# First pair's copy by DMA ahead of the norm, scaled in place; Fourier steps between the chunks of conv1

## The reference

```python
for j in range(4):
    z = conv3x3(x, Kj); z = batchnorm(z, gamma[j], beta[j]); z = relu(z)
    z = conv3x3T(z, Kj)
    x = batchnorm(x + 0.1 * z, gamma[j], beta[j])
    x = diag_imp_conv_fft(x, Lj, 0.1)      # fft2, times a real table per channel, ifft2
```

## Time and profile before

| what | value |
| --- | --- |
| median of 3 runs | 698.69 us (698.69 to 700.88) |
| the profiled execution | 700.2 us, span 698.4 us |
| TensorE (PE) busy | 619.7 us, 89% |
| VectorE (DVE) busy | 493.7 us, 71% |
| ScalarE (ACT) busy | 343.7 us, 49% |
| GpSimd (POOL) busy | 233.3 us, 33% |

### The profile page before, as it was taken

One profiled execution on the slowest core, in us unless ns is written; L12 is line 12 of the kernel. 1 busy time (PEld: TensorE's weight loads), 2 busy tenths in 40 slices (PEclk: granted clock), 3 DMA queues, 4 the chain that ended last, 5 costly groups with the idle time before them and its releaser, 6 DMA issues.

```text
span 698.4 us, 14578 instructions
## 1 busy us (share of the span) xinstructions
PE 619.7 (89%) x5840; PEld 200.9 (29%) x5840; DVE 493.7 (71%) x875; ACT 343.7 (49%) x640; POOL 233.3 (33%) x180
## 2 busy tenths in 40 slices
PE   6498999999999979999898899998978989989783
PEld 4122333222332223233232222332222223323221
DVE  2679888865786785738868767486778554867674
ACT  1466666652894322419932314299223233982232
POOL 0367666771142432202225222022252220222200
PEclk9699999999999999999999999999999999999988
DMA  9995111117600022294000224930004159000044
GB/s 187 182 168 97 32 32 33 31 31 161 157 1 1 1 63 62 70 224 116 1 2 1 70 55 107 224 79 1 2 1 109 30 133 218 3 2 1 1 123 120
DMA packets 44786, 51.21 MB, mean 73 GB/s; under 512 B 36528, under 2 KB 36656, under 8 KB 42672
## 3 DMA queue, kind: packets, MB, share of 16 engines
q1 hardware_dynamic: 40240, 48.99, 32.8%
q10 hardware_dynamic: 4480, 1.30, 1.2%
HBM read 11.99 MB, written 4.19 MB: 23 GB/s over the span
## 4 chain that ended last, share of the span: by engine, by line
PE 54%; ACT 20%; DVE 14%; issue 6%; DMA 3%; SPq 1%; POOL 0%; DVEq 0%; ACTq 0%; POOLq 0%
PE psum L1025 29%; ACT Z L613 10%; PE psum L1097 6%; ACT work L635 6%; PE psum L1164 3%; PE psum L1048 3%; DVE Z L950 2%; DMA X<-X 2%; PE psum L1221 2%; PE psum L1193 2%; PE psum L1236 2%; DVE work L923 2%; PE psum L1085 2%; DVE work L968 2%; DVE work L933 1%
## 5 line engine op out<-in xcount | busy, mean ns | idle before, releaser
L1025 PE MATMUL psum<-X,wts 128*32 128x512 f32 x1536 | 171.3, 594 | 9.1 <-DMA X<-X 5.0
L1025 PE MATMUL psum<-Z,wts 128*32 128x512 f32 x1536 | 172.3, 594 | 4.3 <-DVE Z L890 4.3
L474 POOL TENSOR_TENSOR Z<-X 128x512 f32<-128x512 f32 x64 | 80.8, 1286 | 251.2 <-DVE X L908 251.2
L635 ACT ACTIVATE work<-X,small 128x512 bf16<-128x512 f32 x128 | 90.7, 710 | 87.7 <-DVE X L908 87.7
L550 ACT ACTIVATE Z<-psum 128x512 f32<-128x512 f32 x64 | 38.2, 596 | 140.4 <-PE psum L1025 129.3
L484 POOL TENSOR_TENSOR X<-Z 128x1024 f32<-128x1024 f32 x24 | 56.9, 2394 | 113.0 <-DVE Z L950 113.0
L810 DVE BATCH_NORM_STATS2 stats<-Z 128x6 f32<-128x512 f32 x60 | 41.0, 691 | 69.7 <-ACT Z L550 69.6
L1025 PEld LDWEIGHTS psum<-Z,wts 128*32 128x32 f32 x1536 | 50.1, 109 | 115.5 <-issue 106.9
L613 ACT ACTIVATE Z<-Z,small 128x512 f32<-128x512 f32 (+4 forms) x92 | 80.3, 922 | 5.2 <-DVE small L880 4.7
L1025 PEld LDWEIGHTS psum<-X,wts 128*32 128x32 f32 x1536 | 47.8, 109 | 121.4 <-issue 109.8
L908 DVE SCALAR_TENSOR_TENSOR X<-psum,X 128x512 f32<-128x512 f32 x64 | 44.2, 690 | 36.2 <-PE psum L1025 36.0
(11 more groups left out here) (127 smaller groups left out, 819.5 us busy)
## 6 DMA issues: line engine op xcount, KB each, us to landing
X<-X SPq DMA_DIRECT2D x64, 260.0 KB, 3.9
Z<-Z SPq DMA_DIRECT2D x32, 520.0 KB, 9.2
Z<-x SPq DMA_DIRECT2D x36, 128.0 KB, 4.1
out<-Z SPq DMA_DIRECT2D x24, 128.0 KB, 2.4
parS<-par SPq DMA_DIRECT2D x4, 673.0 KB, 11.8
Z<-x SPq DMA_DIRECT2D x12, 120.0 KB, 5.1
Z<-x ACTq DMA_DIRECT2D x14, 64.0 KB, 4.3
Z<-x SPq DMA_DIRECT2D x14, 64.0 KB, 4.7
```

Of the source, the lines that this page charges most:

```text
L474: nc.gpsimd.tensor_tensor(rows(Z0, REG, bp, CH * (2 * half + i), CH), low, high, op=op)\
L635: nc.scalar.activation(by_row(rest[:, o:o + N // 2].bitcast(bf16)), xc, what, bias=small[:, 26:27], accum_out=sums[:, NCH * i + c:NCH * i ...
L1025: last = nc.tensor.matmul(out_b[C * r:C * r + C, :], weights[:, o:o + C], rows(src, reg, bp, g, CH, dj - 1), start=(dj == 0), stop=(dj == ...
```

## The change

- SP copies pair 0 to X2 (layers 1 to 3) as soon as GpSimd has unmixed it, before the second norm is known, so the copy is unscaled.
- ScalarE then scales X0 of pair 0 in three parts, and with the first and the last the one edge row group of X2 that holds half of the partitions (`scale_first`). VectorE scales the other rows of X2 in three parts (`scale_copy`, steps `copied`). Chunks 0 to 2 of conv1 wait for one part of each.
- conv1 follows the norm and the last two quarters of forward H of pair 2. Inverse W of pair 1 lies ahead of the moments; the return of slot 0 and inverse H of pair 2, and all of pair 3, move between the chunks of conv1.
- In conv2 the return of slot 0 goes behind the following chunk, inverse H of pair 1 and forward W of pair 2 change places, VectorE's scaling becomes a step of its own (`scaled`), and ScalarE's sums of chunks are put off by a table (`SUMS`).
- The weights of conv1 (`prepare((0,))`) are made behind chunk 13 of conv2, those of conv2 in the step `weights`.
- GpSimd's last mixing of a layer waits until the second norm is known.
- The last layer keeps the order behind conv2 (`last_steps`), with the changes in conv2.

```diff
@@ def fourier
     if what == "fwdH":
-        steps = [("slot0", j, bp)] + steps + [("slot0c", j, bp)]
+        steps = [("slot0", j, bp)] + steps + [("scaled", j, bp)]
@@ def layer_steps
-        9: fourier(j, 1, "fwdW"),
+        9: [("slot0c", j, 0)] + fourier(j, 1, "fwdW"),
         10: fourier(j, 0, "invH"),
         11: fourier(j, 1, "fwdH"),
-        12: fourier(j, 0, "invW") + [("back", j, 0)],
-        13: fourier(j, 2, "fwdW"),
-        14: fourier(j, 1, "invH"),
-        15: fourier(j, 2, "fwdH"),
+        12: [("slot0c", j, 1)] + fourier(j, 0, "invW") + [("back", j, 0, 0), ("back", j, 0, 1)],
+        13: fourier(j, 1, "invH"),
+        14: fourier(j, 2, "fwdW"),
...
-    steps += [("moments", j), ("norm", j, 2), ("affine", j, 0), ("turn", j, BP - 1), ("weights", j)]
-    steps += fourier(j, 1, "invW") + [("back", j, 1)] + fourier(j, 3, "fwdW") + fourier(j, 2, "invH")
+    if j + 1 == DEPTH:
+        return steps + last_steps(j)
+    steps += quarters("fwdH", j, 2, (0, 1)) + [("slot0", j, 2), ("scaled", j, 2, 0)] + fourier(j, 1, "invW")
+    steps += [("moments", j), ("norm", j, 2)] + quarters("fwdH", j, 2, (2, 3))
+    steps += [("affine", j, 0), ("copied", j, 0), ("back", j, 1, 0), ("copied", j, 1), ("back", j, 1, 1), ("copied", j, 2)]
+    steps += [("scaled", j, 2, 1), ("turn", j, BP - 1), ("weights", j)]
     rest = {
-        0: [("affine", j, 1)],
-        1: fourier(j, 3, "fwdH"),
-        2: fourier(j, 2, "invW") + [("back", j, 2)],
-        3: fourier(j, 3, "invH"),
-        5: fourier(j, 3, "invW") + [("back", j, 3), ("affine", j, 2)],
+        0: [("slot0c", j, 2)],
+        2: fourier(j, 2, "invH") + [("affine", j, 1)],
+        3: fourier(j, 3, "fwdW"),
+        4: fourier(j, 2, "invW") + [("back", j, 2, 0), ("back", j, 2, 1)],
+        5: fourier(j, 3, "fwdH") + [("affine", j, 2)],
+        6: [("slot0c", j, 3)] + fourier(j, 3, "invH"),
+        7: fourier(j, 3, "invW") + [("back", j, 3, 0), ("back", j, 3, 1)],
         9: [("affine", j, 3)],
     }
+SUMS = {c: (c,) for c in range(5)} | {6: (5,), 8: (6,), 9: (7,), 10: (8,), 11: (9, 10), 12: (11,), 13: (12, 13), 14: (14,), 15: (15,)}
@@ SP
+                        elif bp == 0:
+                            sp.wait_ge(parts_added, 2 * BP * (j - 1) + h + 1)
@@ GpSimd, mix_halves
+                if bp == BP - 1 and i == 1 and j + 1 < DEPTH:
+                    pool.wait_ge(bn_ready, 2 * j + 2)
@@ ScalarE
+            def scale_first(j):
+                for h in range(2):
+                    act.wait_ge(x2_in[0][h], 32 * (j + 2))
+                for g, n in ((0, CH), (CH, CH), (2 * CH, 2 * CH)):
+                    parts = [(X0, REG, g, n, 0, 128)]
+                    if g == 0:
+                        parts.append((X2, REG2, 0, 1, 2 * C, 128))
+                    if g + n == G:
+                        parts.append((X2, REG2, G, 1, 0, 2 * C))
+                    for t, reg, first, many, p0, p1 in parts:
+                        z = rows(t, reg, 0, first, many, 0, p0, p1)
+                        last = nc.scalar.activation(z, z, ACT.Identity, bias=small[p0:p1, 13:14], scale=small[p0:p1, 12:13])
+                    last.then_inc(x_back, n // CH)
@@ VectorE
+            def scale_copy(j, i):
+                dve.wait_ge(bn_ready, 2 * j + 2)
+                for h in range(2):
+                    dve.wait_ge(x2_in[0][h], 32 * (j + 2))
+                g, n = ((1, CH), (1 + CH, CH), (1 + 2 * CH, G - 1 - 2 * CH))[i]
+                z = rows(X2, REG2, 0, g, n)
+                nc.vector.tensor_scalar(z, z, S(12), S(13), ALU.mult, ALU.add).then_inc(copy_scaled, 1)
...
                         dve.wait_ge(bn_ready, 2 * j + 2)
-                        prepare()
+                        prepare((1,))
...
                         elif at[1] == 13 and j + 1 < DEPTH:
                             sum_kernels(j + 1)
+                            prepare((0,))
@@ TensorE
-                    pe.wait_ge(weights_ready, j + 1)
+                    pe.wait_ge(weights_ready, 2 * j if j else 1)
-                if c % Q < 2:
+                if j and c < 3:
+                    pe.wait_ge(x_back, NCH * (j - 1) + (1, 2, 4)[c])
+                    pe.wait_ge(copy_scaled, 3 * (j - 1) + c + 1)
+                elif c % Q < 2:
```

More of the change, by code:

```diff
@@ L156, in layer_steps, with last_steps @@
     for c in range(NCH):
-        if j + 1 < DEPTH:
-            steps.append(("conv1", j + 1, c))
-        steps += rest.get(c, [])
-    return steps
+        steps += [("conv1", j + 1, c)] + rest.get(c, [])
+    return steps
+def last_steps(j):
+    steps = fourier(j, 2, "fwdH") + [("slot0c", j, 2), ("moments", j), ("norm", j, 2), ("affine", j, 0), ("turn", j, BP - 1)]
+    steps += fourier(j, 1, "invW") + [("back", j, 1, 0), ("back", j, 1, 1)] + fourier(j, 3, "fwdW") + fourier(j, 2, "invH")
+    steps += [("affine", j, 1)] + fourier(j, 3, "fwdH") + [("slot0c", j, 3)] + fourier(j, 2, "invW")
+    steps += [("back", j, 2, 0), ("back", j, 2, 1)] + fourier(j, 3, "invH") + fourier(j, 3, "invW")
+    return steps + [("back", j, 3, 0), ("back", j, 3, 1), ("affine", j, 2), ("affine", j, 3)]
+SUMS = {c: (c,) for c in range(5)} | {6: (5,), 8: (6,), 9: (7,), 10: (8,), 11: (9, 10), 12: (11,), 13: (12, 13), 14: (14,), 15: (15,)}
 ORDER = prologue_order()
@@ L169, in number_banks @@
     for step in steps:
-        if step in number or step[0] in ("turn", "back", "affine", "moments", "weights"):
+        if step in number or step[0] in ("turn", "back", "affine", "moments", "weights", "scaled", "copied"):
             continue
@@ L294, in build @@
         parts_added = sem("parts_added")
+        copy_scaled = sem("copy_scaled")
         rows_turned = sem("rows_turned")
@@ L489, in _ @@
                         mix_halves(j, at[1] // Q, at[1] % Q - 2)
-                    elif what == "back" and j + 1 < DEPTH:
-                        unmix_halves(*at)
+                    elif what == "back" and j + 1 < DEPTH and at[2] == 1:
+                        unmix_halves(*at[:2])
         @block.scalar
@@ L647, in scale_x @@
                     act.wait_ge(bn_ready, 2 * j + 2)
+                    if j + 1 < DEPTH:
+                        scale_first(j)
+                        return
                 for h in range(2):
@@ L671, in _ @@
                             relu_pair(j, 3)
-                        sum_x(*at)
+                        for c in SUMS.get(at[1], ()):
+                            sum_x(j, c)
                     elif what == "slot0c":
@@ L698, in sum_kernels, with prepare @@
                                              op=ALU.add, axis=AX))
-            def prepare():
-                for k in range(2):
+            def prepare(some):
+                for k in some:
                     for form in range(2):
@@ L838, in _ @@
                     sum_kernels(0)
-                    prepare()
+                    prepare((0, 1))
                     gamma_and_beta()
@@ L998, in _ @@
                     elif what == "back":
-                        for half in range(2):
-                            move_back(*at, half)
-                    elif what == "slot0":
+                        move_back(*at)
+                    elif what == "copied":
+                        scale_copy(*at)
+                    elif what == "scaled":
                         if at[1] == 0:
                             dve.wait_ge(table_done, 4 * (j + 1))
-                        scale_slot0(*at)
-                    elif what == "fwdH":
-                        scale_fwdH(*at)
+                        if len(at) == 2:
+                            scale_slot0(*at)
+                        for h in at[2:] or (0, 1):
+                            for q in (2 * h, 2 * h + 1):
+                                scale_fwdH(j, Q * at[1] + q)
+                        if at[2:] == [0]:
+                            scale_slot0(j, at[1])
                     elif what == "conv1":
@@ L1148, in conv2 @@
                     pe.wait_ge(relu_done, (2 * BP + 1) * j + 2 * bp + q + 2)
+                if c == 0:
+                    pe.wait_ge(weights_ready, 2 * j + 1)
                 if j == 0 and c == 0:
@@ L1186, in forward_h @@
                 first, q = NUMBER["fwdH", j, c], c % Q
+                if q == 0:
+                    pe.wait_ge(rows_moved, Q * (BP * j + c // Q + 1))
                 for x in range(2):
```

## The result

The changed kernel takes 707.05 us in the median (705.86 to 708.85); the kernel before, run beside it, 699.4. The ratio is 1.0109 with a 95% interval of 1.0076 to 1.0141: slower by 1.1%, where 695.2 was forecast within 687.5 to 703. The profiled execution has a span of 704.2 against 698.4, so 5.8 us longer. Not all of that difference is the change: the stretch ahead of the first conv2 is 1.7 shorter in this profile by chance (table at the head of the experiments), and from there on the changed kernel loses 7.5.

A forecast was written before the change was run, and what follows sets the result against it. TensorE was taken as the bound, busy 125.7 of 136.8 us a layer. Three transitions at 0.4 and the last layer's 2.3 made 3.5 us gained: 696.7 profiled, 695.2 against the median of 698.7, range 687.5 to 703.

The forecast's parts named there:

- The ledger's idle part of a transition: TensorE's waits from conv2 to conv1's end, nine terms summing to 12.2 us after, against 12.6 before including slow clock.
- The wait put at 2.5 us: Forward W of pair 2 waits 2.5 us for moves delayed by conv1's weights beside GpSimd's unmixing; bounds 0 and 3.5.
- the second rival: Port not held behind chunk 13, or both weights done in one turn: the 2.5 goes three times, 687.7; chance 0.17.
- The third rival: GpSimd keeps the port over both unmixing halves, delaying the copy's third piece: 3 x 2.1 us, 701.5; chance 0.07.
- The DMA of the first pair: Copy starts some 10 us before the norm ends and lands within 5, so hidden; otherwise conv1 would wait 4 us.
- one fall a transition: First rival, milder case: clock halves behind one new gap per transition, 3 x 1.7 = 5.1 us, 700.3; chance 0.20.
- two: First rival, double case: clock halves behind both the 2.5 and 2.4 gaps, 10.2 us, 705.4; chance 0.11.
- Its own sign of being wrong: Profile would show a granted clock below 0.95 in the stretches behind the new gaps of 2.5 and 2.4 us.
- the old fall: Half clock behind the 2.6 us wait for the mean slows the inverse transform; its 1.7 us counted as gone.
- The new order in conv2: Waits of 3.7 us removed and 1.3 added in each of four layers: 2.4 gained, if nothing else is late.
- The transition: Each of three transitions, conv2's change included: 12.6 us before, 12.2 after, gain 0.4.
- fourth rival: The step only moves waits: 0.4 is a small difference of large sums, 1 us error gives 692 or 698; no separate chance.

The follow-up runs named there:

- experiment 1: Changed kernel with the kernel sums and conv1's weights made behind chunk 9 of conv2 in place of chunk 13: 699.21 us, ratio 0.9967 to the kernel before.
- Experiment 3: Changed kernel with three extra matmuls, results overwritten, inside each of three TensorE waits of a transition: 699.03 us, ratio 0.997 to the kernel before.
- experiment 8: Changed kernel with three extra matmuls inside the wait ahead of chunk 0 of conv1 alone, no repairs: 703.22 us, ratio 1.0024 to the kernel before.
- experiment 9: Kernel before with three extra matmuls inside its wait for the mean of the second norm: 698.52 us, ratio 0.9954.
- experiment 4: Kernel before with the new order inside conv2 alone; transition, scaled copy, weights and conv1 as before: 693.38 us, ratio 0.9886.
- experiment 6: Changed kernel with weights behind chunk 9, taps behind chunk 10, pair 2's affine behind inverse H 3, and extra matmuls ahead of conv1's chunk 0: 681.71 us, ratio 0.971.
- experiment 5: Changed kernel with sums and weights behind chunk 9, taps behind chunk 10, pair 2's affine step behind inverse H of pair 3: 687.83 us, ratio 0.9781.

## Why the prediction was wrong

**The waits: right, and right in size.** Each of the forecast waits is there, on the engines and behind the instructions named, within 0.3 us. The one not forecast is 0.42. The ledger's idle part of a transition was 12.2; the rows of the table sum to 12.6. The wait put at 2.5 us stands and falls with GpSimd's unmixing (the second rival had it gone): beside the two halves the two weight operations took 2.98 and ended with the second half, with GpSimd idle they took 0.55 and the wait was gone (experiment 1). That a port is what GpSimd holds was the author's assumption, and no run shows one. The third rival (the third piece of the copy held up over both halves) did not come: the piece took 0.76, begun at 392.67, and GpSimd's operation, begun at 392.82, 0.08 behind the transposes that released it, took 2.74, where the two behind chunk 13 took 2.38 and 2.39. The DMA of the first pair was hidden, chunk 4 did not wait.

**The step that failed is the clock.** The prediction put 0.20 on one fall a transition and 0.11 on two, and took none in its sum. Its own sign of being wrong, a clock below 0.95 behind the new gaps, came at 0.79 and 0.76. There were five falls in three transitions: 3 x 1.6 behind the scaled copy, and two of about 1.7 elsewhere (inverse W 3 shows 1.4 of its own, the chunks behind it 0.3), some 8 us. Experiment 3 filled the waits without shortening them; the falls went, and 8.1 us of the three transitions with them. Two errors stand behind it. First, the pair of windows in the earlier trace rows showed one gap that lost the clock and one that didn't, and the text took it as likely that most of the new gaps keep it. But in that same trace the clock fell at the norm in every transition, and the new order puts three gaps of that size in each where there had been one. That more such gaps make a fall surer is argued, not shown; what is shown is that five of nine lost it here, and that with one gap of each transition filled (experiment 8) three of the other six did, where it had been two. Second, the ledger booked the old fall, 1.7 a transition, as time that the change wins back. It did leave, but experiment 9 shows that it had been in the shadow of VectorE's chain. The sum is not harmed by that, as the idle time beside it would have been 1.7 longer; the judgement is, since the new falls lie where TensorE sets the pace and have no shadow.

**A smaller term was put at nothing.** Experiments 9 and 3 are the two kernels at full clock in every transition: 409.9 before, 413.1 after. So even without a fall the three transitions are 3.2 longer, where the ledger had them 1.2 shorter, an error of 1.5 in each. Layer 1 of both, from conv2 to conv2, experiment 9 first:

```profile
316.60:453.20 136.60, 125.57 (x1242) 40.41 (x1242) 96.37 (x171) 65.05 (x121) 39.17 (x24) 1.00 0.30 69
317.30:454.90 137.60, 129.42 (x1254) 41.97 (x1254) 99.97 (x174) 66.43 (x125) 39.88 (x24) 1.00 0.29 68
```

Less the extra matmuls (1.56 a wait, one wait and three) TensorE works 124.0 and 124.7, and is idle or filled for 12.6 and 12.9. The 0.7 of work was in no term: the prediction took the work of TensorE as given. The new order cuts it into more pieces, and a chunk by itself shows 2.78 where one inside a run takes 2.65; that this makes the 0.7 is likely and was not tested. All together, for the profiles: 8.1 for the falls and 3.2 at full clock, less 1.9 by which the kernel before is longer than that of experiment 9 (1.6 of it at the DMA), make 9.4 for the transitions; less 1.9 in the last layer 7.5; less the 1.7 ahead of the first conv2 the 5.8 between the spans.

**The gain in conv2 is there, somewhat smaller.** The new order in conv2 was put at 2.4 us a layer and gives 8 in four layers by the medians (experiment 4), 1.8 a layer where the profiles show it undisturbed. The transition was put at a gain of 0.4 without falls, a small difference of large sums (fourth rival), and lost 1.1. Its three new waits are each accidents of place, and not of the idea: with them repaired the idea is worth 1.05% of ratio beyond the conv2 order alone, and 1.8% with the clock held (8.3 and 11.4 us in the transitions of the profiles).

What stays open: in which of its gaps of 2.2 to 2.4 us a given kernel loses the clock, and why the third layer's wait for the DMA is 2.7 or 2.8 in two profiles of the old transition (the kernel before, experiment 4) and 1.1 in the third (experiment 9).

## What to carry to other kernels

When work is moved between an engine's steps, write down for each step what it waits for and, for VectorE's, what GpSimd is doing at that time (the two weight operations took 2.98 us beside it and 0.55 without); three instructions at the wrong place (two weight operations beside an unmixing, the taps ahead of four moves, an affine step ahead of a copy) cost 5.9 us of waits in each transition here, and moving them by a few chunks took 5.3 of it away. A TensorE gap such as those of 2.2 to 2.4 us here can have two prices, its length and the half clock behind it (1.6 to 1.7 us here), and the second was only paid where TensorE set the pace. It was had back here by three matmuls whose results nobody reads.

## What the runs showed of the hardware that was not expected

- Matmuls of 1.56 us inside a wait of 2.4 us were enough to keep the full clock (1.00 in all three transitions of experiments 3 and 6). The clock's two levels show in the same 24 matmuls: 2.78 us at a granted clock of 1.00, 4.39 at a mean of 0.62 (1.00 first, then 0.50), 5.35 at 0.50 throughout (third transition of experiment 1).
- Of waits of 2.42 us with the same work ahead of them, all three lost the clock in the changed kernel, and two of three in experiment 5.
- A fall cost 1.7 us or nothing by where it lay: in the last layer it was hidden in a wait for VectorE or reached the work behind it (103.4 against 105.0).
- A VectorE operation on 96 columns with two inputs in SBUF took up to 2.45 us beside GpSimd, and 0.30 alone (changed kernel, at 398.0, just after GpSimd's unmixing had ended). Behind chunk 13 in layer 1 the first of two ended 0.1 after GpSimd's first operation (0.63), the second 0.1 after the next one (2.43). The row over the whole span of the changed kernel (least, median, most, in ns):

```profile
L746 DVE SCALAR_TENSOR_TENSOR wts<-ksum,cstS,parS x16: 304/624/2446, 56.7 to 539.3; 128x96 f32<-128x96 f32 x16
```
